# A recurrence, two attentions and a routed feed-forward: keys loaded inside the recurrence, and work of each next stage moved ahead of its barrier

## The reference, cut to what matters

```
r = sigmoid(i_r + h_r); z = sigmoid(i_z + h_z); n = tanh(i_n + r * h_n)
h_new = (1 - z) * n + z * h                       # GRU, 256 steps in series
q, k, v = x @ Wq + bq, x @ Wk + bk, x @ Wv + bv   # causal attention, 16 heads of 128
out = softmax(q k^T * scale + mask) v @ Wo + bo
x = x + attention(gru(cond, x))
xn = rms_norm(x, g_norm) * (1 + scale) + shift    # scale, shift from emb, by batch
q, k, v = xn @ W_qkv                              # 16 heads of 16; q and k are rms-normed
y = o + o @ W_out
shared = silu(y Wg) * (y Wu) @ Wd * sigmoid(y @ gate_vec)
routed = sum over the top 4 of 16 experts, weighted by the normed softmax
x = x + shared + routed
```

## Time and profile before

| what | value |
|---|---|
| median of 3 runs | 1015.22 us (1012.39 to 1018.44) |
| the profiled execution's own time | 1017.57 us |
| its span, first to last instruction | 1015.7 us |
| TensorE busy, share of the span | 951.5 us, 94% |
| VectorE, ScalarE, GpSimd busy | 694.0, 593.7, 574.4 us |

### The profile page before, as it was taken

How to read it: one execution, slowest core, us unless ns; L and a number is a source line. 1 busy time by engine, 2 the same in 40 slices (tenths; PEclk the granted TensorE clock), 3 DMA queues, 4 the chain that set the end, 5 groups by cost and what they waited for, 6 DMA issues and landing times. The chain is left out here.

```text
span 1015.7 us, 37730 instructions
## 1 busy us (share of the span) xinstructions
PE 951.5 (94%) x15031; PEld 760.6 (75%) x15031; DVE 694.0 (68%) x2755; ACT 593.7 (58%) x2044; POOL 574.4 (57%) x1260
## 2 busy tenths in 40 slices
PE   3899999999999999998999999778888999999997
PEld 3799999999999999986888888545445565666664
DVE  5887777777777777775766667758863566656665
ACT  4666666666666666666777777657783433333332
POOL 2677766666666666665777765277003365556552
PEclk8555555555555555559999999999996999999999
DMA  9110111111111111113222231010000144334331
GB/s 366 46 23 15 25 24 25 25 24 17 22 25 25 25 25 24 18 21 101 71 72 72 88 130 40 1 41 1 2 2 16 32 127 125 116 109 125 127 112 42
DMA packets 79802, 58.99 MB, mean 58 GB/s; under 512 B 64886, under 2 KB 70776, under 8 KB 79116
## 3 DMA queue, kind: packets, MB, share of 16 engines
q1 hardware_dynamic: 79628, 56.58, 19.5%
HBM read 47.33 MB, written 8.98 MB: 55 GB/s over the span
## 5 line engine op out<-in xcount | busy, mean ns | idle before, releaser
L558 POOL COPY gp<-hq 128x16 f16<-128x16 f16 x256 | 68.2, 266 | 151.2 <-DVE hq L522 151.1
L598 POOL TENSOR_TENSOR q_part<-q_raw,q_part 128x64 f16<-128x64 f32 x238 | 113.6, 477 | 19.3
L335 PE MATMUL gq<-gp,wq_part 128*128 128x64 f16 x1428 | 121.1, 242 | 0.0
L1962 POOL TENSOR_SCALAR w_hi<-wf_ffn 128x512 f16<-128x512 f32 (+1 forms) x56 | 29.7, 530 | 158.5 <-POOLq L1182 69.6
L263 PE MATMUL gr<-hq,w_one 128*128 128x4 f16 x2048 | 118.0, 166 | 0.0
L319 PE MATMUL gq<-gp,raws 128*128 128x64 f16 x1440 | 115.3, 236 | 0.0
L596 POOL CAST q_part<-q_raw 128x64 f16<-128x64 f32 x238 | 111.8, 470 | 0.4
L1888 ACT ACTIVATE h_hi<-hT 128x512 f16<-128x512 f32 x56 | 35.3, 630 | 130.0 <-DVE hT L1940 130.0
L373 ACT ACTIVATE r_scan<-gr 128x8 f32<-128x8 f32 x256 | 46.3, 181 | 110.7 <-PE gr L263 110.6
L335 PEld LDWEIGHTS gq<-gp,wq_part 128*128 128x128 f16 x1428 | 94.9, 132 | 0.0
L263 PEld LDWEIGHTS gr<-hq,w_one 128*128 128x128 f16 x2048 | 94.1, 104 | 0.0
(11 more groups left out here) (271 smaller groups left out, 2955.8 us busy)
## 6 DMA issues: line engine op xcount, KB each, us to landing
wf_ffn<-in_wf SPq DMA_DIRECT2D x28, 384.0 KB, 3.1
k_kept<-k_made SPq DMA_DIRECT2D x60, 128.0 KB, 2.8
kh<-k_kept SPq DMA_DIRECT2D x16, 480.0 KB, 3.6
raw_attn<-in_pairs SPq DMA_DIRECT2D x8, 770.0 KB, 4.4
cw_of<-cw_rows SPq DMA_DIRECT2D x9, 512.0 KB, 3.4
shared<-in_wq SPq DMA_DIRECT2D x1, 2056.0 KB, 11.0
q_part<-in_wk SPq DMA_DIRECT2D x1, 2048.0 KB, 15.0
cw_of<-cw_rows SPq DMA_DIRECT2D x4, 448.0 KB, 3.6
```

What stands on the lines that cost most here:

```text
L335: mm = pe.matmul(q_bank[t % 2][:, 0:B * QB].rearrange("p (b t) -> p b t", b=B), wq_part[:, w, c, j * P:(j + 1) * P], gp[:, g, j, :, h * QB ...
L558: nc.gpsimd.tensor_copy(gp[:, :, :, :, t].rearrange("p q j b -> p q (j b)"), hq[:, nxt, :, 2::3]).then_inc(h_stored, 1)
L598: nc.gpsimd.tensor_tensor(q_part[:, 1, h, :, :, c], src, q_part[:, 0, h, :, :, c], ALU.subtract).then_inc(q_split, 1)
```

## The change

The change touches all three borders between blocks.

1. `kh` is allocated ahead of both first blocks and holds `x_part` until the recurrence has read it. SP loads two heads' keys ahead of the last set's stores; of these two stores one is now issued by ScalarE. The last step makes no query, so `left` has 19. One filler less at the end of the recurrence, and the four in the attention's start are gone. Value groups 2 and 3 move into unit 0. The bias matmuls move from unit 1 to unit 2. The table for exponentials is loaded ahead of the first value copy.
2. The squares of batches 1 to 3 move into the norm's block. The rows of batch 0 are scaled, transposed, conditioned and split in the attention's block. The fillers around this go. GpSimd's fills are halved, and the fill of `v` moves behind the tiles.
3. In the norm's block GpSimd splits the feed-forward's chunk 0 and `y` of batches 0 to 2; TensorE makes their gate and logits in steps 20, 22 and 24 (`ahead_of_ffn`), and ScalarE reads them. From step 20 the weights use four banks, not five. The gate is a tanh with a scale and an offset, and the exponential's table is loaded in step 7. In the feed-forward only the last batch is left, and the routing is spread over half chunks 0 to 2 (`routed`).

```diff
-        x_part = sb("x_part", [P, 2, J, B, T], FP16)
+        x_part = kh[:].rearrange("p e q h n -> p (e q h n)").rearrange("p (w j b t) -> p w j b t", w=2, j=J, b=B)
...
+                if n == (T - QB) // KSET - 1:
+                    sp.wait_ge(k_out[0], 16 * (T - QB) // KSET)
+                    sp.wait_ge(r_psum, T - QB + 1)
+                    for h in range(2):
+                        load_keys(sp, kh, k_kept, k_in, h)
...
+                keep(sp, n, 0)
+                if n < (T - QB) // KSET - 1:
+                    keep(sp, n, 1)
...
+            act.wait_ge(k_lo, T - QB)
+            keep(act, (T - QB) // KSET - 1, 1)
...
             keys(0, first_keys)
             first_group(0)
-            keep_busy(pe, S[0][:], w_part("v", 0, 0)[:, 0:P], w_part("v", 0, 0)[:, 0:HALF], 4)
             pe.wait_ge(k_ready, 1)
             pe.wait_ge(k_in[0], 16)
             scores(0)
             first_group(1)
-            first_group(2)
-            first_group(3)
...
+                if u == units + 2:
+                    for i in range(TC):
+                        x_turned(i)
...
                     else:
-                        pe.wait_ge(v_ready, B)
+                        first_group(2)
                     pe.wait_ge(p_ready, u + 1)
                     turned(u)
+                    if u == 0:
+                        first_group(3)
...
-                if u == 1:
+                if u == 2:
                     pe.wait_ge(bo_ready, 1)
...
+            keep_busy(pe, TB[:], w_part("o", H1 // 2 - 1, 0)[:, 0:P], w_part("o", H1 // 2 - 1, 0)[:, 0:HALF], 3)
...
+            nc.scalar.activation(root[:], ones[0:1, 0:1], ACT.Exp)
             first_value_hi(0)
...
+                if u == units - 1:
+                    act.wait_ge(adaln["eps_ready"], 2)
+                    act.wait_ge(adaln["ss_ready"], TC)
+                    nc.scalar.activation(adaln["rms"][:, 0:TC], adaln["ss"][:, 0:TC], ACT.Sqrt,
+                                         bias=adaln["epst"][:, 0:1], scale=1.0 / D).then_inc(adaln["rms_ready"], 1)
...
+                if u == units - 2:
+                    nc.scalar.activation(root[:], ones[0:1, 0:1], ACT.Sqrt)
+            for i in range(TC):
+                act.wait_ge(adaln["xt_psum"], i + 1)
+                for j in range(J):
+                    nc.scalar.activation(x32[:, i, j, :], x_bank[i][:, j * P:(j + 1) * P],
+                                         ACT.Identity, bias=adaln["emb"][:, J + j, 0:1],
+                                         scale=adaln["gain"][:, j, 0:1]).then_inc(adaln["x32_ready"], 1)
...
+            def scaled():
+                dve.wait_ge(adaln["rms_ready"], 1)
+                nc.vector.reciprocal(adaln["rstd"][:, 0:TC], adaln["rms"][:, 0:TC]).then_inc(adaln["rstd_ready"], 1)
+                dve.wait_ge(adaln["rstd_ready"], 1)
+                for i in range(TC):
+                    nc.vector.tensor_scalar(xn[:, i, :], x1[:, i, :], adaln["rstd"][:, i:i + 1], None,
+                                            ALU.mult).then_inc(adaln["xn_ready"], 1)
...
+                if u == units:
+                    scaled()
+                    finished(1)
...
-                if u >= units - 2 and u < units:
-                    finished(u - units + 2)
+                if u == units - 2:
+                    finished(0)
+                    squared()
             finished(2)
+            dve.wait_ge(adaln["x32_ready"], J)
+            nc.vector.tensor_copy(rows["x_hi"][:, :, 0:P], x32[:, 0]).then_inc(adaln["xhi_ready"], 1)
             finished(3)
...
+            def ahead_of_ffn(b):
+                pe.wait_ge(turn_read, turn_of["y", b] + 1)
+                if b:
+                    pe.wait_ge(ffn["lg_read"], b)
+                else:
+                    kind, n = last[4]
+                    pe.wait_ge(mx_done if kind == "score" else exp_done, n + 1)
+                    pe.wait_ge(ffn["w_in"], 48)
+                for j in range(J):
+                    pe.matmul(bk[4][:, 0:T], ffn["gv"][:, j, :], yT[:, j, batch_cols(b)],
+                              start=(j == 0), stop=(j == J - 1))
+                for tc in range(TC):
+                    for j in range(J):
+                        mm = pe.matmul(bk[4][:, T + tc * E:T + (tc + 1) * E], yT[:, j, tile_cols(b * TC + tc)],
+                                       ffn["gw"][:, j, :], start=(j == 0), stop=(j == J - 1))
+                mm.then_inc(y_in, 1)
...
-            busy(x_bank, 5)
-            x_turned(0)
-            busy(qk_banks[0], 3)
-            x_turned(1)
...
+                if t == TILES - 1:
+                    nc.scalar.activation(rms[0:1, 0:1], ident[0:1, 0:1], ACT.Exp)
...
+                b = (t - AHEAD - 1) // 2
+                if (t - AHEAD) % 2 == 1 and 0 <= b < B - 1:
+                    act.wait_ge(y_in, b + 1)
+                    nc.scalar.activation(ffn["gate"][:, batch_cols(b)], bk[4][:, 0:T], ACT.Tanh, scale=0.5)
+                    nc.scalar.activation(ffn["lg"][:, b * TC:(b + 1) * TC, :].rearrange("p i e -> p (i e)"),
+                                         bk[4][:, T:T + TC * E], ACT.Copy).then_inc(ffn["lg_read"], 1)
...
+                if t in (0, 2):
+                    squared(t // 2 + 2)
+                if t in (1, 3):
+                    scaled(t // 2 + 2)
...
-            nc.gpsimd.memset(q_rows[:, :, :, 3 * SLOT:], 0.0).then_inc(pads, 1)
-            rest(0)
+            nc.gpsimd.memset(q_rows[:, 0:TILES // 2, :, 3 * SLOT:], 0.0).then_inc(pads, 1)
             rest(1)
-            nc.gpsimd.memset(k_rows[:, :, :, 3 * SLOT:], UNIT).then_inc(pads, 1)
-            nc.gpsimd.memset(v[:, :, :, DH2:], 1.0).then_inc(pads, 1)
+            nc.gpsimd.memset(k_rows[:, 0:TILES // 2, :, 3 * SLOT:], UNIT).then_inc(pads, 1)
+            nc.gpsimd.memset(q_rows[:, TILES // 2:, :, 3 * SLOT:], 0.0).then_inc(pads, 1)
+            nc.gpsimd.memset(k_rows[:, TILES // 2:, :, 3 * SLOT:], UNIT).then_inc(pads, 1)
...
+            pool.wait_ge(ffn["wf_in0"], 16)
+            temp = qk[:].rearrange("p a n -> p (a n)")
+            split_chunk(nc, pool, ffn, 0, temp[:, 0:6 * P], y_temp, 0)
+            pool.wait_ge(v_psum, TILES)
+            pool.wait_ge(ffn["gu_ready"], 1)
+            pool.wait_ge(ffn["d_ready"], 1)
+            for b in range(B - 1):
+                cols = batch_cols(b)
+                raw = temp[:, 0:J * T].rearrange("p (j t) -> p j t", j=J)
+                pool.wait_ge(turn_read, turn_of["y", b] + 1)
+                if b:
+                    pool.wait_ge(ffn["y_ready"], 2 * b)
+                nc.gpsimd.tensor_scalar(x_hi[:, :, cols], yT[:, :, cols], YS, 0.0, ALU.mult, ALU.add)
+                nc.gpsimd.tensor_scalar(raw, yT[:, :, cols], YS, 0.0, ALU.mult, ALU.add).then_inc(y_temp, 1)
+                pool.wait_ge(y_temp, 3 + b)
+                nc.gpsimd.tensor_tensor(x_lo[:, :, cols], raw, x_hi[:, :, cols],
+                                        ALU.subtract).then_inc(ffn["y_ready"], 1)
+                pool.wait_ge(ffn["lg_read"], b + 1)
+                nc.gpsimd.tensor_scalar(ffn["gate"][:, cols], ffn["gate"][:, cols], 0.5, 0.5,
+                                        ALU.mult, ALU.add).then_inc(ffn["y_ready"], 1)
...
-            for i in range(TILES):
+            for i in range(TILES - TC, TILES):
                 for j in range(J):
...
+                if u == 0:
+                    pe.wait_ge(y_ready, 4)
+                if u == 1:
+                    pe.wait_ge(y_ready, 6)
+                    pe.wait_ge(y_lo_ready, 1)
...
+                if u < 3:
+                    routed(u + 1)
```

More of the change, by code:

```diff
@@ new lines, with split_chunk @@
+WFS, YS = 64.0, 16.0
+def split_chunk(nc, pool, a, c, big, written, made):
+    par = c % 2
+    for n, (cols, ready) in enumerate(((slice(0, 4 * P), a["gu_ready"]), (slice(4 * P, 6 * P), a["d_ready"]))):
+        if "free" in a and c >= 2:
+            pool.wait_ge(a["free"][n], 2 * (c - 2) + 2)
+        nc.gpsimd.tensor_scalar(a["w_hi"][:, par, cols], a["wf"][:, par, cols], WFS, 0.0, ALU.mult, ALU.add)
+        nc.gpsimd.tensor_scalar(big[:, cols], a["wf"][:, par, cols], WFS, 0.0,
+                                ALU.mult, ALU.add).then_inc(written, 1)
+        pool.wait_ge(written, made + n + 1)
+        nc.gpsimd.tensor_tensor(a["w_lo"][:, par, cols], big[:, cols], a["w_hi"][:, par, cols],
+                                ALU.subtract).then_inc(ready, 1)
@@ L1827, in _ @@
             mm.then_inc(lg_psum, 1)
-            for hf in range(2):
-                for j in range(J):
-                    mm = pe.matmul((MB, UB)[hf][:], gv[:, j, :], yT[:, j, halves[hf]],
-                                   start=(j == 0), stop=(j == J - 1))
-                mm.then_inc(gate_psum, 1)
+            for j in range(J):
+                mm = pe.matmul(MB[:, 0:T], gv[:, j, :], yT[:, j, last], start=(j == 0), stop=(j == J - 1))
+            mm.then_inc(gate_psum, 1)
             for u in range(units):
@@ L1863, in _ @@
         def _(act):
```

(13 more changed lines are left out.)

300 lines of the change are left out of this document (162 added, 138 removed).

## The result

The changed kernel took 1006.39 us in the median of seven executions (1003.81 to 1010.03), the kernel before 1014.68 (1012.39 to 1018.44) beside it: ratio 0.9919, 95% interval 0.9896 to 0.9941. Six more executions on another chip gave 0.9924 (0.9908 to 0.9941); 0.991 to 0.993 had been expected of them, and 0.995 if the first seven had been lucky with the clock. That is 8.3 us less, where 11.3 were forecast. One execution of the kernel before took 2618.92 us and is left out of the ratios.

What follows compares the result with a forecast made beforehand. TensorE's nearly gapless feed-forward loop was taken as the bound, so starting it earlier gains. Terms -1.4 - 5.4 - 0.7 + 4.5 - 8.3 = -11.3 us, from the 1015.22 median, gave 1003.9 us; own range 1001 to 1007, full range 997 to 1010.

Steps and rivals of the forecast that it cites:

- The bound and the sign: Feed-forward loop on TensorE stays unchanged at 3.9 us a half chunk and starts earlier; faster, chance 0.87.
- rival 2: Norm's tiles and steps: GpSimd and VectorE block each other, extra matmuls wholly exposed; 1007.4 us, chance 0.20.
- Border one, -1.4: Recurrence to attention: earlier stage start -0.5, earlier second unit's inverse -1.9, bias matmuls no longer hidden +1.0.
- -2.4 if they hide again: First border's lower bound: -2.4 us if the 1.04 us of bias matmuls fall in a wait again.
- Border two, -5.4: Attention to norm: earlier stage start, GpSimd's first tile sooner, +1.5 for collisions in the tiles; range -6.9 to -4.0 us.
- so it starts the first tile at 665.15: Norm's start: GpSimd's own work takes 5.0 us from 660.15, so its first tile starts then, against 672.07.
- stop GpSimd for their length: Norm's tiles: upper bound 2.9 us if four squares and four scalings on VectorE stop GpSimd; the middle, +1.5, was taken.
- Table, -0.7: Norm's block: loading the exponential's table two steps earlier, where ScalarE waits, saves 0.7 us (0 to -1.3).
- Router's and gate's work, +4.5: Norm's late steps: gate and logit matmuls of batches 0 to 2 add 4.5 us on TensorE (+2.0 to +5.6).
- Border three, -8.3: Norm to feed-forward: logits and gate take 3.4 us against 12.4, with clock terms +1.7 and -1.0; range -5.6 to -11.1.
- VectorE has room in them, and the weights of the experts are used later: 0: Feed-forward's start: spreading the routing over three units costs nothing.
- rival 1: Third border: TensorE's clock stays up, logits and gate take 1.9 us, 4.3 us less in all; 999.6 us, chance 0.17.

Runs made afterwards that it cites:

- the one with fillers: The kernel before with ten fillers of 512 columns in the waits of the last steps of the norm's stage; ratio 0.9991.

## Why the prediction was right, and where its sizes were off

- **The bound and the sign.** Nothing behind the third border moved (195.2 us in each profile), and all the time came from the borders, as said. The time lies in the range; the sum was 3 us too large. By the stretches it was 2.8 too large in border two and 1.1 in border three, and the other terms erred by 1.1 the other way; that part is luck. So is that the median lies nearer to rival 2's 1007.4 than to 1003.9: that rival's steps (tiles 1.4 longer than taken, the extra matmuls wholly exposed) did not happen.
- **Border one, -1.4.** Measured -1.66 in the stretch. Behind the last state the second unit's inverse is 2.7 earlier (0.5 + 1.9 forecast), the third unit's transposition too. The bias matmuls give back 1.04 in the unit behind it: the fourth unit's transposition (476.63, in before 477.69) is 1.6 earlier behind the last state. No scores wait for a transfer. The bound "-2.4 if they hide again" is what the run with the bias matmuls in unit 1 gave (192.93 against 195.29).
- **Border two, -5.4: the term that was too large.** Stage's start -1.07 (behind the last inverse) where I had -0.8; tiles +0.74; but GpSimd's first tile came 7.80 behind the start, not 5.0. The step that failed is "so it starts the first tile at 665.15": it counts GpSimd's own work and no wait for VectorE. I had priced the collision in the tiles, at half of what four squares and four scalings would cost if they "stop GpSimd for their length", that is, as VectorE stopping GpSimd. The tiles lost 0.74 and not 1.5. The larger loss is the other way: GpSimd's instructions stop VectorE (3.67 for 0.62), and what waits behind VectorE's scaling is the tile's own sums. The run with one wait added wins 2.1 of the 2.8 back. The earlier trace rows had the case in it, 2.18 for 0.62 beside one fill. -2.6 against the other executions of before, -3.6 against the profiled one.
The Trainium skill ("SBUF — State Buffer", Who interferes with whom) has the shared ports go to whichever of the two issues first, for one instruction. That agrees with the rows as far as it goes: GpSimd's subtraction had started at 660.66, 0.08 ahead of the scalings. But the first scaling alone lasted 3.41 us, to behind the last of the three fills that followed that subtraction: it was not let in between them, and for that no run here shows a reason.
- **Table, -0.7.** Measured -0.85.
- **Router's and gate's work, +4.5.** Measured +3.84 (52.72 to 56.55). By the timeline 0.6 of it is no matmul: at 731.69 a VectorE instruction of 0.24 us takes 1.24 beside GpSimd's new subtraction, and TensorE waits for it:

```profile
731.68 1.16 POOL L1814 TENSOR_TENSOR wq_part<-qk,wq_part 128x512 f16<-128x512 f32 x1
731.69 1.24 DVE L1693 SCALAR_TENSOR_TENSOR q_rows<-mx,q_rows 128x16 f16<-128x16 f32 x1
...
732.99 0.62 PE L1415 MATMUL turn<-ident,q_rows 128*128 128x128 f16 x8 [0.58 <-DVE q_rows L1693]
```

- **Border three, -8.3.** -7.2 against the second execution of before, -9.0 against the profiled one and another -2.1 in the tail. Two errors lie in it. The work that left was priced at 12.4 us, which holds for an execution whose clock fell early; the second spent 10.6, and the one with fillers 9.0. And the start of the feed-forward loses 1.4 us (first product to seventh `prod` 27.74, in before 26.33). Its first `prod` stands 3.95 behind the first product, in the second profile of before 2.81. Little of that is the silu, whose table load (776.74) now comes last on ScalarE: it starts 2.40 behind the first product, in before 2.11. The `prod` could have started when the silu was done, at 778.6, but VectorE had the last batch's routing to finish (the MAX8 row at 778.68) and came to it at 779.58. So the step that failed here is "VectorE has room in them, and the weights of the experts are used later: 0". In before the whole routing lay beside TensorE's gate products and was over at 790.8, ahead of the first `prod` at 792.7. This is read from the timeline; no run moved the routing. The first product stands 1.84 behind the stage's start and not 3 to 4, for the clock stayed up in the profiled execution, as rival 1 had it, and fell in others. Even so that execution took 1004.68 and not rival 1's 999.6.
- **The sum.** With the second execution of before: -2.1 - 1.1 - 2.3 + 0.8 - 1.3 + 2.7 + 0 - 7.2 = -10.5, the difference of the spans (1013.4 to 1002.9). The medians differ by 8.3; I put the rest down to the clock in the changed kernel's other executions, of which one has a profile.

Left open: how much of the spread that remains at one mean clock comes from the loads at the program's start (the last state stands between 456.8 and 457.9 in all the profiles, whatever the kernel), and whether the executions without a profile had their low clock where the profiled ones had it.

## What to carry to other kernels

A price read from one execution holds its clock: before a stage's cost goes into a sum, look at the granted clock over it, and cut a second execution into the same stretches. When work is moved onto a GpSimd that looked idle, ask which VectorE instruction now runs beside it and who waits behind that one: 0.3 us of scaling became 3.4, and one added wait won 2.1 us. When the work that covered another engine's chain goes, look for that chain's next cover: the routing, free beside the gate products, held the first `prod` for 0.9 us. Work that must be somewhere belongs in a wait of its own engine: the router's matmuls cost 1.08 us ahead of the last values and nothing in the gaps right behind; the bias matmuls cost 1.04 us in one unit and 0.3 in the one before.

## What the hardware did that I had not expected

- The mean granted clock of two executions of before was 0.992 and 0.994 where others had 0.77, for spans of 1014.5 and 1012.9 against 1010.8 to 1017.0. Three executions of other kernels did the same (0.994 to 0.997). The recurrence, which ran at 0.52 in the profiled ones, shows no gain from 2.4 GHz; none of these executions has a profile.
- The low clock came behind a wait in one place and not in another: after 2.23 us without work TensorE ran at 0.57 for 3.7 us, and a run of 16-column matmuls that kept it busy without a gap was followed by 0.51. With the same gate matmuls mixed between them it stayed at 1.00. Each of these stands in one profile.
- A VectorE scaling of 0.31 us was held for 3.41 us, behind one GpSimd subtraction and three fills in a row, which read nothing; with a wait between them the pair took 1.00 and not 3.67.
